# Decoder layer, cross-attention: value products of three pairs in groups of three tiles instead of two

## The reference

```python
q = (x @ Wq).reshape(B, S, HEADS, DIM_HEAD).transpose(0, 2, 1, 3)      # 8 heads of 64
k = (context @ Wk).reshape(B, L, HEADS, DIM_HEAD).transpose(0, 2, 1, 3)
v = (context @ Wv).reshape(B, L, HEADS, DIM_HEAD).transpose(0, 2, 1, 3)
attn = jnp.einsum('bhsd,bhld->bhsl', q, k) * scale
attn = jax.nn.softmax(attn, axis=-1)
out = jnp.einsum('bhsl,bhld->bhsd', attn, v)
out = out.transpose(0, 2, 1, 3).reshape(B, S, INNER)
return out @ Wo + bo
```

## Time and profile before

| what | us |
|---|---|
| median of 3 runs | 1288.47 |
| lowest, highest | 1286.87, 1291.5 |
| the profiled execution | 1291.7 |
| its span, first to last instruction | 1290.0 |
| TensorE busy | 1172.4 |
| VectorE busy | 725.9 |
| GpSimd busy | 715.3 |
| ScalarE busy | 592.1 |

### The profile page before, as it was taken

One profiled execution on the slowest core, in us unless ns is written; L12 is line 12 of the kernel. 1 busy time (PEld: TensorE's weight loads), 2 busy tenths in 40 slices (PEclk: granted clock), 3 DMA queues, 4 the chain that ended last, 5 costly groups with the idle time before them and its releaser, 6 DMA issues.

```text
span 1290.0 us, 18849 instructions
## 1 busy us (share of the span) xinstructions
PE 1172.4 (91%) x6456; PEld 685.7 (53%) x6456; DVE 725.9 (56%) x1297; ACT 592.1 (46%) x1031; POOL 715.3 (55%) x617
## 2 busy tenths in 40 slices
PE   3789797879999999999999999999999999999991
PEld 2456464545555555555555555555554466566661
DVE  7686867662466744657835556835665654423222
ACT  5676767624445643545543545444443423222222
POOL 2284656325587775678785776875766132422222
PEclk9899999979999999999999999999998999999996
DMA  6009700001000000100000100000003742332324
GB/s 200 17 9 337 254 2 1 1 1 26 1 1 1 26 1 2 42 1 1 26 34 1 43 1 26 9 26 17 1 1 130 262 103 43 74 45 46 47 37 143
DMA packets 38926, 65.75 MB, mean 51 GB/s; under 512 B 4129, under 2 KB 31393, under 8 KB 38561
## 3 DMA queue, kind: packets, MB, share of 16 engines
q1 hardware_dynamic: 25792, 49.45, 12.0%
q0 software_dynamic: 7152, 9.38, 4.4%
q10 hardware_dynamic: 5888, 5.72, 1.7%
HBM read 50.96 MB, written 30.61 MB: 63 GB/s over the span
## 4 chain that ended last, share of the span: by engine, by line
PE 74%; DVE 15%; issue 4%; ACT 4%; DMA 2%; ACTq 1%; another core or an unknown queue 0%; POOL 0%; SPq 0%; DVEq 0%; POOLq 0%
PE PS L1896 16%; PE PS L1907 12%; PE PS L1783 10%; PE PS L1973 9%; DVE mxp L1511 5%; PE PS L1991 5%; PE PS L1802 3%; PE PS L227 3%; PE PS L1694 2%; PE PS L1704 2%; PE PS L228 2%; PE PS L229 2%; PE PS L1683 2%; PE PS L1982 1%; PE PS L1877 1%
## 5 line engine op out<-in xcount | busy, mean ns | idle before, releaser
L732 POOL TENSOR_TENSOR acc<-acc,PX 128x1024 f32<-128x1024 f32 (+1 forms) x165 | 392.9, 2381 | 127.5 <-ACT PX L1012 118.8
L1012 ACT ACTIVATE PX<-PS 128x1024 f32<-128x1024 f32 (+1 forms) x208 | 212.5, 1026 | 261.9 <-PE PS L1896 256.3
L1511 DVE TENSOR_REDUCE mxp<-PS 128x2 f32<-128x804 f32 x256 | 243.1, 990 | 127.1 <-PE PS L1802 126.2
L1907 PE MATMUL PS<-PX,V 128*64 128x512 f32 (+1 forms) x832 | 209.4, 613 | 0.2 <-ACT PX L1012 0.2
L787 POOL DMA_INDIRECT Y<-yb,goal_u x39 | 60.8, 1558 | 183.6 <-DVE yb L1600 144.2
L1973 PE MATMUL PS<-W,XBT 128*128 x312 | 147.1, 594 | 1.6 <-issue 0.8
L664 POOL TENSOR_SCALAR_AFFINE_SELECT A<-A 128x128 f32<-128x128 f32 x256 | 85.4, 350 | 111.2 <-ACT A L899 108.3
L899 ACT ACTIVATE A<-PS 128x512 f32<-128x512 f32 (+3 forms) x256 | 97.7, 445 | 65.0 <-PE PS L1694 63.8
L1896 PE MATMUL PS<-QH,KH 64*128 64x512 f32 (+1 forms) x416 | 102.3, 488 | 4.8 <-ACT PX L1012 3.2
L1896 PEld LDWEIGHTS PS<-QH,KH 64*128 64x128 f32 (+1 forms) x416 | 38.1, 179 | 117.9 <-issue 81.3
L1907 PEld LDWEIGHTS PS<-PX,V 128*64 128x64 f32 (+1 forms) x832 | 48.6, 137 | 79.1 <-issue 73.2
(11 more groups left out here) (293 smaller groups left out, 2105.5 us busy)
## 6 DMA issues: line engine op xcount, KB each, us to landing
W<-in_w SPq DMA_DIRECT2D x24, 512.0 KB, 4.8
XB<-XG ACTq DMA_DIRECT2D x39, 130.0 KB, 2.1
X<-in_x SPq DMA_DIRECT2D x1, 2048.0 KB, 12.0
Y<-X SPq DMA_DIRECT2D x4, 512.0 KB, 3.4
X<-Y SPq DMA_DIRECT2D x4, 512.0 KB, 5.5
out<-X SPq DMA_DIRECT2D x8, 256.0 KB, 2.1
xt_raw<-in_xt SPq DMA_DIRECT2D x3, 512.0 KB, 3.9
c_raw<-in_ctxt SPq DMA_DIRECT2D x6, 200.0 KB, 2.7
```

What stands on the lines that cost most here:

```text
L732: ins = pool.tensor_tensor(sums[0:r], sums[0:r], PX[0:r, (NL * p + t) % NP, :, :], ALU.add)
L1012: act.activation(PX[0:r, u % NP, :, :], PS[0:r, score_buffer(u):score_buffer(u) + 2, :], ACT.Exp, scale=XD ** -0.5)\
L1511: dve.tensor_reduce(mxp[:, p % 2, :, v % NT, v // NT:v // NT + 1].rearrange("p a o -> p (a o)"), PS[:, k:k + 2, 0:BW], AX, ALU.max)\
L1907: mm = pe.matmul(PS[rows, 4, :], V[0:LROWS[j], j, P * p + XD * half:P * p + XD * half + XD], PX[0:LROWS[j], u % NP, half, :], start=(j == ...
```

## The change

One table. Value products of pairs two to four stood two by two at the ends of slots 2, 4, 6, 8 and 10, with tile 10 alone in slot 11; now tiles 0 to 2 stand in slot 3, 3 to 5 in slot 6, 6 to 8 in slot 9, and 9 and 10 in slot 11. Tiles 11 and 12 stay in slot 0 of what follows. No instruction is added or removed, and the queues of the other engines keep their order.

```diff
-        VALUES_LATER = {2: [0, 1], 4: [2, 3], 6: [4, 5], 8: [6, 7], 10: [8, 9], 11: [10]}
+        VALUES_LATER = {3: [0, 1, 2], 6: [3, 4, 5], 9: [6, 7, 8], 11: [9, 10]}
```

## The result

The changed kernel takes **1306.63 us** (median of 4 runs, 1305.76 to 1308.61) against 1288.69 for the kernel before on the same chip: ratio 1.0143, interval 1.0122 to 1.0164, so 17.9 us slower. The sign was as forecast, the size was not: +9.7 was forecast, and the time lies just above the range of 1291.5 to 1306.

The account below looks back on a forecast made before the run. TensorE, busy 91% of the span, was taken to bound the kernel. Savings of 4.3 us, added waits and what pair borders give back summed to +9.7 us, 1298.2 by the median of 1288.47; range 1291.5 to 1306.

Parts of the forecast that it names:

- slot 8: Emptied of value products, it waits for the score-exponential loop: 0.8 us per plain pair, 0.13 with transposes, together +4.0.
- Slot 10: TensorE waits for VectorE's maxima: +4.2 us in four plain pairs, +3.0 in pair three, -1.8 in two pair fours.
- The hold of the `PX` buffers: Exponentials of tiles 4, 7, 10 await buffers freed by a group's first tile; they end before three tiles do: no cost.
- Batch four: Lost cover and waits in pair three, and a later end of pair four: together +5.8 us.
- the count matmuls of pair three: In batch four, value products that covered VectorE's delay before these matmuls now come after them: +1.9 us.
- The last pair, with the attention's end: Batch four's pair four: the end comes 1.8 us later; with 0.4 counted as saved there, +2.2.
- The 0.15 for a group's start: Each value group costs 0.15 us besides 0.86 per tile; 24 groups fewer save 3.6 us.
- Slots 3, 6, 9 ... no cost: Groups of three value tiles at these slots delay no following scores, which come 0.6 us later than they must: 0.
- Pair four, slots 3 to 5: Batches two and three: next key product waits 0.6 us for VectorE's split, slot 5 loses 0.2 of cover: +1.6 together.
- the stream stays dense (2): Rival: slots without value products are not short, so only the -4.3 us saving is left, 1284; chance 0.06.
- waits and savings cancel (3): Rival: costs of slot 10 and batch four are given back at pair borders, +1.3 us, 1290; chance 0.12.
- Rival (4): Waits bring TensorE's clock down: two or three more half-clock stretches add 5 to 10 us, 1303 to 1308; chance 0.12.

Follow-up runs that it names:

- e1_slot8: Kernel before with only the value products of tiles 6 and 7 moved, from slot 8 to slot 9: 1303.10 us, ratio 1.0075.
- e3_slots2to6: Kernel before with only tiles 0 to 2 put at slot 3 and 3 to 5 at slot 6: 1300.58 us, ratio 1.0058.
- e5_maxima_high: Changed kernel with slot 3's row maxima waiting only for the rounded keys, not the whole split: 1303.64 us, ratio 1.0099 to the kernel before.
- e10_batch4_only: Kernel before with the new table of value products in batch four alone: 1301.21 us, ratio 1.0063.
- e2_slot10: Kernel before with only tiles 8 and 9 moved, from slot 10 to slot 11: 1303.44 us, ratio 1.0083.

## Why the prediction was right in sign and short in size

**What held.** The loop bare of value products is 2.30 to 2.34 in slot 8 of all ten pairs. Slot 10 waits 0.91 for VectorE in plain pairs; in pair three it is 0.33 and then 0.58 for the split, together what was forecast. The hold of the `PX` buffers costs nothing with three tiles, and e1_slot8 shows by its 0.36 how near the bound was. Batch four came out near its sum, in part by luck: around the count matmuls of pair three, where 1.9 was forecast, slot 8 cost 0.8 and the wait went from 1.50 to 1.70, slot 6 cost 0.7 where 1.2 was forecast, and slot 3 cost 0.3 where nothing was. The pair grew by 3.7 with a stretch at half clock in both traces; in the changed kernel's third trace, which has none there, the pair is 3.2 shorter. How the rest divides between waits and clock is not shown. The last pair, with the attention's end, grew by 1.3, forecast 1.8 to 2.2. The 0.15 for a group's start stands in the new rows as well: three tiles 2.72, two 1.87. By the Trainium skill (TensorE: Matmul & The Clock Gate, "Step-by-step: what each phase is for") the next weights load while the matmul before still runs. If a group's start were free by that, three tiles would take 2.58 (an estimate, 3 x 0.86); the rows of this kernel say otherwise.

**The step that failed.** "Slots 3, 6, 9 ... no cost". The step looked at one thing that could be late, the buffer hold, and not at what stands next in slot 3: the maxima wait for VectorE's split of the first key part. In the kernel before, 1.87 of value products in slot 2 lay between. The prediction saw this cover for pair four, under "Pair four, slots 3 to 5", and took it to be that pair's alone, with the next key product as the one to wait; it is the maxima that wait, in pairs two to four alike (the last pair of all has no maxima). Slots 2 to 6 cost 0.3 to 0.36 in seven pairs of the row where nothing was forecast, 0.6 in pair four of batch one, and 1.58 (forecast 0.8) in two. e3_slots2to6 shows the place, e5_maxima_high the cause: undoing this wait alone gave back 4.0 in the slots and about 5 in the median. A second wait that the sum lacked is small: in pair three the projection of slot 9 waits for VectorE's split of the transposes, 0.2 in each of three, 0.6 in all.

**The term left small.** The clock was a rival with a chance of 0.12 and no term in the sum. Within one program the mean granted clock and the span go together: over 96 executions under eleven labels, each taken against the mean of its own label, 0.001 less clock goes with 0.84 us more (correlation -0.89). The changed kernel's eleven executions have a mean clock of 0.9684, those of the kernel before (37) 0.9703: 1.6 us of the 3.0 that the medians show beyond the 14.9. For e10_batch4_only (0.9658, with 0.9694 for the kernel before in the same session) the same relation gives 3.0 of its 8.1 and leaves 5.1, against the 5.0 of its slots. That is a relation between numbers, not an experiment on the clock; I made none that holds the clock fixed. In the first trace of the changed kernel the stretches at half clock inside the attention came to 10.2 us, as many as before, and only their places moved.

**What stays open.** About 1.4 us of the 17.9, for which the traces show no place in the attention, what sets off a stretch at half clock in one execution and not in the next, and why the wait in the expert part is 0, 1.7 or 2.45 long.

**The rivals.** That the stream stays dense (2) and that waits and savings cancel (3) are refuted: slots 8 and 10 wait in all three traces of the changed kernel, and the time is 17.9 above before. Rival (4) gave 1303 to 1308 and the time lies there, but for another reason in the main: by the relation above the clock accounts for about 2, by e5_maxima_high the maxima's wait for 4 to 5. Its added stretches came in the kernels with parts of the change (e1_slot8, e2_slot10, e3_slots2to6, e10_batch4_only), not in the changed kernel's own traces.

## What to carry to other kernels

When work is moved out of a slot, don't ask only what the moved work itself waits for; go through each wait that stands behind the gap, in every repetition of the loop, and subtract the moved time from its slack. Here the waits of slots 8 and 10 were costed to some tenths, and those of slot 3, behind the emptied slot 2, were not looked at. A wait that is removed tells nothing until the next one on the engine is known: moving the loads took away 1.31 and brought 2.34. And where a short loop runs beside, filler in single tiles can hide in a turn of it, even at 0.15 a group, if the turn has no other work: in the last pair it made slots of 2.31 with a tile in them, but of 3.01 where a projection stood too.

## What the runs showed of the hardware

The slots of the kernel before repeat within 0.2 us in two traces, most of them within some hundredths, but the stretches at half clock do not stay in place. The same program at the same slot, first and third trace of the changed kernel, windows and timeline of TensorE for each:

```profile
990.00:994.00 4.00, 4.00 (x12) 1.76 (x14) 0.45 (x3) 1.02 (x1) 0.05 (x1) 0.50 0.00 0
```

```profile
989.40 1.45 PE L1829 MATMUL PS<-tally,ones 128*128 128x8 f32 x6 [1.70 <-DVE X L1538]
990.78 5.39 PE L1907 MATMUL PS<-PX,V 128*64 128x512 f32 x12
```

```profile
990.00:994.00 4.00, 3.31 (x18) 1.52 (x18) 1.08 (x5) 1.02 (x1) 0.27 (x1) 1.00 0.00 0
```

```profile
990.68 0.83 PE L1829 MATMUL PS<-tally,ones 128*128 128x8 f32 x6 [1.70 <-DVE X L1538]
991.45 2.79 PE L1907 MATMUL PS<-PX,V 128*64 128x512 f32 x12
```

The same 1.70 of idle time stands ahead of both, and the group takes 5.39 in one and 2.79 in the other. In the third trace a stretch lies instead at the end of pair two of batch two, where slots 10 to 12 take 9.64 in place of 7.95. A slot's length at half clock is thus no property of the slot; a forecast should give such stretches as a number per attention, with a spread: the three attentions of the changed kernel took 748.09, 747.88 and 745.15.
